# Output projection of the first batch's tokens at the end of the attention part, the rest in four banks

## The chip, the cores and the metric

The kernel runs on one core of one Trainium2 chip. The metric is the device time of one launch in microseconds; lower is better. The kernel before has a median of 1011.29 us over three runs (1010.05 to 1013.51).

## What is computed

One transformer layer on x of shape (2, 1024, 512): a layer norm, causal attention with 16 heads of 32, a mixture of 8 experts with the top 2 per token, and both results added to x. Cut to what matters here:

```python
xn = layernorm(x)
q, k, v = split(xn @ w_attn + b_attn); rope on q and k (by head index)
attn = softmax(where(causal, q @ k.T, -inf)) * 512 ** -0.5
a = (attn @ v) @ w_proj + b_proj                     # output projection
probs = softmax(xn @ gate_w.T); top 2 experts per token, weights normalised
f = sum over the two experts: w * (silu(g) * u) @ w2, with g, u = split(xn @ w1)
out = x + a + f
```

## The kernel before

The program has three parts, each a block: at the end of a block all five engines meet, and none starts the next part before the last has come.

`project_qkv` computes the layer norm, q, k, v and the router's choice and stores them in HBM. `attend` is the attention. It runs 16 rounds (`ROUNDS`), each for two heads of one batch: rounds 0 and 1 belong to batch 0, 2 and 3 to batch 1, and so on through four groups of heads; four heads of one batch make a span, of which there are 8 (`SPANS`). A round has 12 steps (`NS`); in each PE computes a block of transposed scores (`scores`), ACT takes the exponential into `probs`, and PE multiplies by the values (`values`) into `o_acc`. In steps 0 to 3 and 8 to 11 the block lies on the diagonal, and GpSimd sets what is above it to zero first (line 1137); the value product waits for that (`masked`). Beside this PE computes the scores once more for the round two ahead (`unit`), of which DVE takes the row maxima. SP issues all transfers of this part: the loads of q, k and v three rounds ahead (`load`, lines 1019 and 1023), the rows of maxima (`rows`, 1030), the sums and unscaled outputs of a finished round (`sort_out`, 1041 and 1045), and for each span the sums back in (`load_totals`, 1052), the shares, which DVE makes of them with a reciprocal (`share`, 1215), out (`store_shares`, 1056) and spread over partitions (`spread_shares`, 1064). GpSimd then scales the span's outputs in `o_t` (`scale_span`, 1129), in odd rounds behind the mask of step 3, and for the last span behind the last round. SP's order within a round is written out by hand: load, second half's `sort_out` of the round before, spreading, rows, totals, first half's `sort_out`, store of shares.

`experts` begins with the output projection. `o_t` holds the attention's output transposed, 16 token tiles of 128. For each tile `a` SP loads x's rows into one of 4 buffers `res` (708), GpSimd adds the bias (729), PE multiplies by `w_proj` in 4 steps, each two matmuls in the profile (887), into the bank `gu[a % 2][0]`, DVE adds the two (801) back into `o_t`, and SP stores that to `acc` in HBM (712). PE may start tile `a` when DVE is through with tile `a - 2`. ACT issues the weights of expert `e`, three transfers (788 to 790), when `3e - 1` tiles are done (16 at most):

```python
if e:
    act.wait_ge(res_done, min(3 * e - 1, NT))
if e == E - 2:
    rows_to_sbuf(0, 0)
```

ACT does its first expert work only behind the last of these issues. GpSimd waits for the weights of all 8 experts in turn (`expert_ready`), only then loads the first tag (`load_tag`, 737: a token's number and weight), and waits for the 16 stores before the first accumulation.

Then come 39 expert tiles (`SLOT_TILES`) of 128 routed rows: load of rows (702), transposition (PE 830, ACT 764), up projection (PE 835), silu (ACT 779), product (DVE 818), transposition (PE 845, DVE 808), down projection (PE 853), scaling by the tag (ACT 771), and accumulation into `acc` by an indirect DMA (747). Tile `i` of ACT starts with `y_to_sbuf(i - 2)`, which waits for tag `i - 2`, and ends with the silu of tile `i` and the rows of tile `i + 1`; PE turns the hidden values of tile `i - 1` within tile `i`. At the end SP copies `acc` to the output.

## Time and profile before

| | |
|---|---|
| median of three runs | 1011.29 us |
| profiled execution | 1012.41 us |
| its span, first to last instruction | 1010.8 us |
| PE busy | 881.2 us (87%) |
| DVE busy | 360.9 us (36%) |
| ACT busy | 291.1 us (29%) |
| GpSimd (POOL) busy | 282.7 us (28%) |
| mean granted clock of PE | 0.931 |
| moved by DMA | 143.12 MB, mean 142 GB/s |
| part 1, `project_qkv` | 0 to 190 us |
| part 2, `attend` | 190 to 608 us |
| part 3, `experts` | 608 to 1011 us, its projection to 668 us |

The profiled execution is 1.1 us above the median; its span leaves out 1.6 us around the first and the last instruction. Shares of busy time are means over the three parts, which have different limits, so the timeline and the stretches are to be read part by part. In the rows, SPq and ACTq are DMA issues by SP and ACT, PEld is PE's weight load, and what stands in brackets is the idle time before a group and what ended it.

### The profile page before, as it was taken

The page shows a single profiled execution, that of the slowest core. Times are in us where ns is not written, and L with a number is a line of the kernel's source. Part 1 is how long each engine was busy: PE and PEld are TensorE (multiplying, and loading weights), DVE is VectorE, ACT ScalarE, POOL GpSimd, SP SyncE. Part 2 cuts the span into 40 slices and gives each one's busy share as a digit, 9 for nine tenths or more (in the row PEclk, how much of TensorE's full clock was granted, in tenths as well). Part 3 has the DMA queues.
Part 4 walks back from the last instruction along what each step waited for, and adds up shares of the span by engine and source line. Part 5 has one row for each costly group of instructions (what it writes and reads, how often), then busy time and mean ns, then how long its engine had stood idle before and what let it go on. Part 6 is the DMA issues. An engine that isn't in the chain of part 4 may idle for free. (4 is left out here: it accounts for less than half of the span.)

```text
span 1010.8 us, 12520 instructions
## 1 busy us (share of the span) xinstructions
PE 881.2 (87%) x3533; PEld 524.8 (52%) x3534; DVE 360.9 (36%) x1086; ACT 291.1 (29%) x612; POOL 282.7 (28%) x363
## 2 busy tenths in 40 slices
PE   3899999375999889898989938999999999999990
PEld 2768778243554445455545413445566666656650
DVE  5853342572566555565655101111111111111110
ACT  2221121001465445454544620011222222222210
POOL 5732300466011221212122122413222333222231
PEclk9989999756799899999999978999999999999995
DMA  9296595998176554566651018994333333333326
GB/s 327 112 290 208 188 302 186 220 291 291 34 126 113 90 111 86 106 132 120 105 106 39 25 48 308 372 352 103 73 62 62 62 62 66 67 75 63 62 31 187
DMA packets 107415, 143.12 MB, mean 142 GB/s; under 512 B 46192, under 2 KB 54896, under 8 KB 107312
## 3 DMA queue, kind: packets, MB, share of 16 engines
q1 hardware_dynamic: 82864, 93.74, 36.3%
q0 software_dynamic: 9424, 18.69, 10.3%
q10 hardware_dynamic: 15088, 30.22, 9.0%
q8 instruction: 17, 0.28, 0.1%
q14 instruction: 22, 0.18, 0.1%
HBM read 79.11 MB, written 59.06 MB: 137 GB/s over the span
## 5 line engine op out<-in xcount | busy, mean ns | idle before, releaser
L1172 ACT ACTIVATE probs<-scores_t 128x512 f32<-128x512 f32 (+3 forms) x384 | 163.5, 490 | 149.6 <-PE scores_t L1280 127.5
L835 PE MATMUL gu<-w,rows_t 128*128 x624 | 197.6, 459 | 1.7 <-ACT rows_t L764 1.6
L1257 PE MATMUL maxima<-k_stack,q_stack 96*128 96x512 f32 (+3 forms) x384 | 145.1, 401 | 35.7 <-DVE row_lo L1207 19.8
L1298 PE MATMUL o_acc<-probs,v_ones 128*64 128x512 f32 (+3 forms) x768 | 152.2, 519 | 12.4 <-POOL probs L1137 12.4
L835 PEld LDWEIGHTS gu<-w,rows_t 128*128 128x128 f32 x624 | 115.0, 190 | 70.8 <-issue 21.1
L1280 PE MATMUL scores_t<-q_stack,k_stack 98*128 98x512 f32 (+3 forms) x384 | 141.9, 397 | 6.2 <-ACT probs L1172 3.3
L1193 DVE CUSTOM_DVE_ANT_0 masked_scores<-maxima,mask_m 128x128 f32<-128x128 f32 (+3 forms) x256 | 120.6, 486 | 38.7 <-PE maxima L1257 32.3
L1197 DVE TENSOR_REDUCE mx<-maxima 128x1 f32<-128x512 f32 x128 | 88.2, 689 | 115.4 <-PE maxima L1257 106.9
L1257 PEld LDWEIGHTS maxima<-k_stack,q_stack 96*128 96x128 f32 x384 | 80.1, 211 | 59.7 <-DVE row_lo L1207 24.4
L1280 PEld LDWEIGHTS scores_t<-q_stack,k_stack 98*128 98x128 f32 x384 | 75.1, 199 | 64.2 <-issue 45.3
L853 PE MATMUL down<-w,hidden_t 128*128 (+1 forms) x234 | 107.0, 592 | 0.8 <-DVE hidden_t L809 0.8
L1137 POOL TENSOR_SCALAR_AFFINE_SELECT probs<-probs 128x256 f32<-128x256 f32 x120 | 48.2, 408 | 192.8 <-ACT probs L1172 192.5
L1298 PEld LDWEIGHTS o_acc<-probs,v_ones 128*64 128x64 f32 x768 | 48.0, 140 | 80.6 <-issue 41.5
L808 DVE COPY hidden_t<-hid_ps 128x256 f32<-128x256 f32 x39 | 16.6, 425 | 178.6 <-PE hid_ps L845 178.6
L771 ACT ACTIVATE y<-down,tag 128x512 f32<-128x512 f32 x39 | 26.8, 687 | 184.2 <-PE down L853 153.0
L887 PE MATMUL gu<-w_proj,o_t 128*128 128x512 f32 x128 | 58.3, 617 | 18.3 <-POOL ident L724 17.9
L747 POOL DMA_INDIRECT acc<-y,tag x39 | 64.0, 1640 | 16.8 <-issue 16.5
L853 PEld LDWEIGHTS down<-w,hidden_t 128*128 128x128 f32 (+1 forms) x234 | 44.5, 190 | 46.4 <-issue 38.4
L746 POOL TENSOR_TENSOR carrier_y<-ident 128x1 f32<-128x1 f32 x39 | 7.4, 190 | 192.4 <-ACT y L771 192.4
L495 PE MATMUL bank<-xt_hi,w_hi 128*128 128x512 f32 x128 | 52.3, 408 | 4.8 <-DVE w_lo L355 4.8
L818 DVE TENSOR_TENSOR hidden<-gu,gated 128x352 f32<-128x352 f32 x39 | 20.5, 525 | 92.3 <-PE gu L835 84.2
L737 POOL DMA_DIRECT2D tag<-routed x39 | 46.1, 1182 | 23.9 <-DMA w<-in_w_t 23.9
(147 smaller groups left out, 860.3 us busy)
## 6 DMA issues: line engine op xcount, KB each, us to landing
w<-in_w_t ACTq DMA_DIRECT2D x8, 1408.0 KB, 7.4
routed<-blank_row ACTq DMA_DIRECT2D x20, 514.0 KB, 6.2
rows<-routed SPq DMA_DIRECT2D x39, 256.0 KB, 4.1
qk_hi<-st_hi SPq DMA_DIRECT2D x32, 256.0 KB, 4.2
qk_lo<-st_lo SPq DMA_DIRECT2D x32, 256.0 KB, 5.3
q_stack<-qk_hi SPq DMA_DIRECT2D x32, 256.0 KB, 4.3
k_stack<-qk_hi SPq DMA_DIRECT2D x32, 256.0 KB, 6.6
x_rows<-xn SPq DMA_DIRECT2D x4, 1024.0 KB, 5.1
```

Source lines behind the costliest of these rows:

```text
L495: nc.tensor.matmul(out, a_hi(k), b_hi(k), start=(k == 0), stop=False)
L747: pool.indirect_dma_start(out=scratch["acc"], out_offset=bass.IndirectOffsetOnAxis(ap=tag[:, r, 0:1].bitcast(U32), axis=0), in_=y[:, r, :] ...
L835: last = nc.tensor.matmul(gu[r][j][:, 0:I], rows_t[r][:, k * P:(k + 1) * P], w1[:, bass.ds(e, 1), k, j * I:(j + 1) * I].rearrange("p o n - ...
L853: last = nc.tensor.matmul(down[r][:], hidden_t[r][0:n, k, :], w2[0:n, bass.ds(e, 1), k, :].rearrange("p o n -> p (o n)"), start=(k == 0), ...
L887: last = nc.tensor.matmul(gu[a % 2][0][:], o_t[:, g, a * P:(a + 1) * P], wp[:, g, :], start=(g == 0), stop=(g == NG - 1))
L1137: nc.gpsimd.affine_select(out=p, in_=p, compare_op=ALU.is_ge, fill=0.0, base=0, pattern=[[0, PAIR], [1, P]], channel_multiplier=-1).then_i ...
L1172: nc.scalar.activation(probs[:, k % PR, h, 0:w], scores_t[e % RING][:, 0:w], ACT.Exp).then_inc(exp_done, 1)
L1193: nc.vector.tensor_tensor_reduce(out=masked_scores[bank][:, 0:w], in0=scores, in1=mask_m[:, CH - w:CH], scale=1.0, scalar=NEG, op0=ALU.add ...
L1197: nc.vector.tensor_reduce(to, scores, AX.X, ALU.max).then_inc(m_free, 1)
L1257: nc.tensor.matmul(mb[at % RING][:, 0:w], q_st[i][0:3 * HD, h, t * P:(t + 1) * P], k_st[i][0:3 * HD, h, c * CH:c * CH + w], start=True, st ...
L1280: last = nc.tensor.matmul(out[:, 0:w], k_st[i][0:STACK, h, j * P:(j + 1) * P], q_st[i][0:STACK, h, t0:t0 + w], start=True, stop=not diag)
L1298: last = nc.tensor.matmul(o_acc[c][2 * HD * h:2 * HD * (h + 1), CH - w:CH], v_st[i][:, j, h, :], probs[:, k % PR, h, 0:w], start=(j == 0), ...
```

## The change

The first batch's 8 token tiles (`EARLY`) are projected in `attend`, behind the last value products, into the six banks that scores and maxima used (`proj_banks`). They belong to spans 0, 2, 4 and 6, so PE waits for 7 scaled spans. The bias and x of this batch are loaded in round 7 (`ROUNDS // 2 - 1`) with two transfers on SP's queue; x goes over the place of the normalised rows, which have been scattered by then. GpSimd adds the bias to one tile in each of rounds 8 to 15, before step 4. DVE adds and SP stores each tile; the reciprocal of the last span comes behind DVE's first addition. In `experts` 8 tiles (`LATE`) are left, in four banks; all weights from expert 3 on are issued when all 8 are done.

```diff
@@ -39,6 +39,7 @@
 CLEAR_TILES = -(-SLOT_TILES // (NCH * CLEARS)) * NCH * CLEARS
+EARLY = S // P
 I_TILES = [(0, 128), (128, 128), (256, 96)]
...
@@ -645,6 +646,7 @@
         RES = 4
+        LATE = NT - EARLY
         res = m.sbuf("res", [P, RES, D], F32)
...
@@ -665,7 +667,8 @@
         tag_in = [m.sem(f"tag_in{r}") for r in range(2)]
-        acc_started, added, stored = m.sem("acc_started"), m.sem("added"), m.sem("stored")
+        acc_started = keep["acc_started"]
+        added, stored = m.sem("added"), m.sem("stored")
         carried = m.sem("carried")
...
@@ -703,13 +706,14 @@
             tile(1, 1, 0)
-            for a in range(NT + RES - 1):
-                if a < NT:
-                    sp.dma_start(res[:, a % RES, :], x_rows[a]).then_inc(res_in[a % RES], 16)
+            for a in range(LATE + RES - 1):
+                if a < LATE:
+                    sp.dma_start(res[:, a % RES, :], x_rows[EARLY + a]).then_inc(res_in[a % RES], 16)
                 if a >= RES - 1:
                     done = a - (RES - 1)
+                    at = EARLY + done
                     sp.wait_ge(res_done, done + 1)
-                    sp.dma_start(acc_rows[done], o_t[:, :, done * P:(done + 1) * P]).then_inc(acc_started, 16)
+                    sp.dma_start(acc_rows[at], o_t[:, :, at * P:(at + 1) * P]).then_inc(acc_started, 16)
             run_tiles(sp, tile, 2)
...
@@ -724,7 +728,7 @@
             pool.wait_ge(bp_in, 16)
-            for a in range(NT):
+            for a in range(LATE):
                 pool.wait_ge(res_in[a % RES], 16 * (a // RES + 1))
...
@@ -782,8 +786,8 @@
                 if e:
-                    act.wait_ge(res_done, min(3 * e - 1, NT))
-                if e == E - 2:
+                    act.wait_ge(res_done, min(3 * e - 1, LATE))
+                if e == E // 2:
                     rows_to_sbuf(0, 0)
...
@@ -794,11 +798,12 @@
         def _(dve):
-            for a in range(NT):
+            for a in range(LATE):
+                at = EARLY + a
                 dve.wait_ge(proj_full, a + 1)
                 dve.wait_ge(biased, a + 1)
 
-                nc.vector.tensor_tensor(o_t[:, :, a * P:(a + 1) * P], gu[a % 2][0][:].rearrange("p (g t) -> p g t", t=P),
+                nc.vector.tensor_tensor(o_t[:, :, at * P:(at + 1) * P], gu[a % 2][a // 2 % 2][:].rearrange("p (g t) -> p g t", t=P),
                                         res[:, a % RES, :].rearrange("p (g t) -> p g t", t=P), ALU.add).then_inc(res_done, 1)
...
@@ -868,7 +873,7 @@
                 else:
-                    pe.wait_ge(res_done, NT - 1 + i)
+                    pe.wait_ge(res_done, LATE)
                 pe.wait_ge(expert_ready, e + 1)
...
@@ -878,13 +883,14 @@
             pe.wait_ge(ident_done, 1)
-            for a in range(NT):
-                if a >= 2:
-                    pe.wait_ge(res_done, a - 1)
-                if a == NT - 1:
+            for a in range(LATE):
+                at = EARLY + a
+                if a >= 4:
+                    pe.wait_ge(res_done, a - 3)
+                if a == LATE - 1:
                     turn_rows(0, 0, 0)
                 for g in range(NG):
-                    last = nc.tensor.matmul(gu[a % 2][0][:], o_t[:, g, a * P:(a + 1) * P], wp[:, g, :],
+                    last = nc.tensor.matmul(gu[a % 2][a // 2 % 2][:], o_t[:, g, at * P:(at + 1) * P], wp[:, g, :],
                                             start=(g == 0), stop=(g == NG - 1))
...
@@ -953,10 +959,14 @@
         o_t = keep["o_t"]
+        res = keep["x_rows"][:, 0:EARLY, 0:D]
+        bp = m.sbuf("bp_early", [P, D], F32)
 
         scores_t = [m.psum(f"scores_t{r}", [P, CH]) for r in range(RING)]
         o_acc = [m.psum(f"o_acc{c}", [P, CH]) for c in range(NC)]
         mb = [m.psum(f"maxima{r}", [P, CH]) for r in range(RING)]
+
+        proj_banks = scores_t + mb
 
...
@@ -976,6 +986,9 @@
         scaled = m.sem("o_scaled")
+        bp_in, res_in, biased = m.sem("bp_early_in"), m.sem("res_early_in"), m.sem("biased_early")
+        proj_full, res_done = m.sem("proj_early_full"), m.sem("res_early_done")
+        acc_rows = scratch["acc"][0:T, :].rearrange("(a p) (g t) -> a p g t", p=P, t=P)
         LOADS = 6 + PAIR
...
@@ -1068,6 +1081,10 @@
             for n in range(ROUNDS):
+                if n == ROUNDS // 2 - 1:
+                    sp.wait_ge(scattered, 16 * TOPK * NT)
+                    sp.dma_start(bp[:], b_proj.partition_broadcast(P)).then_inc(bp_in, 16)
+                    sp.dma_start(res, x[0].rearrange("(a p) d -> p a d", p=P)).then_inc(res_in, 16)
                 if n + SETS - 1 < ROUNDS:
...
@@ -1085,6 +1102,9 @@
             spread_shares(SPANS - 1)
+            for a in range(EARLY):
+                sp.wait_ge(res_done, a + 1)
+                sp.dma_start(acc_rows[a], o_t[:, :, a * P:(a + 1) * P]).then_inc(keep["acc_started"], 16)
 
...
@@ -1138,6 +1158,12 @@
                         scale_span(n // PAIRS - 1)
+                    if k == TPC and n >= ROUNDS - EARLY:
+                        a = n - (ROUNDS - EARLY)
+                        if a == 0:
+                            pool.wait_ge(bp_in, 16)
+                            pool.wait_ge(res_in, 16)
+                        nc.gpsimd.tensor_tensor(res[:, a, :], res[:, a, :], bp[:], ALU.add).then_inc(biased, 1)
             scale_span(SPANS - 1)
...
@@ -1233,7 +1259,13 @@
                     join(n + UNITS_AHEAD)
-            share(SPANS - 1)
+            for a in range(EARLY):
+                dve.wait_ge(proj_full, a + 1)
+                dve.wait_ge(biased, a + 1)
+                nc.vector.tensor_tensor(o_t[:, :, a * P:(a + 1) * P], proj_banks[a % len(proj_banks)][:].rearrange("p (g t) -> p g t", t=P),
+                                        res[:, a, :].rearrange("p (g t) -> p g t", t=P), ALU.add).then_inc(res_done, 1)
+                if a == 0:
+                    share(SPANS - 1)
 
...
@@ -1331,6 +1363,19 @@
                         values(n, k)
+
+            pe.wait_ge(w_proj_in, 16)
+            pe.wait_ge(scaled, SPANS - 1)
+            pe.wait_ge(exp_done, ROUNDS * NS * PAIR)
+            pe.wait_ge(m_free, ROUNDS * NU)
+            pe.wait_ge(row_lo_done, ROUNDS)
+            for a in range(EARLY):
+                if a >= len(proj_banks):
+                    pe.wait_ge(res_done, a - len(proj_banks) + 1)
+                for g in range(NG):
+                    last = nc.tensor.matmul(proj_banks[a % len(proj_banks)][:], o_t[:, g, a * P:(a + 1) * P], keep["w_proj"][:, g, :],
+                                            start=(g == 0), stop=(g == NG - 1))
+                last.then_inc(proj_full, 1)
 
...
@@ -1353,6 +1398,7 @@
             "tile_expert": m.sbuf("tile_expert", [1, SLOT_TILES], I32),
+            "acc_started": m.sem("acc_started"),
         }
```

On SP, from the store of shares in round 6 to the sums of round 6 in round 7, behind which comes the spreading of shares, it is now (before, without the rows of lines 1086 and 1087):

```order
L1069 DMA shares_all<-shares 128x32
L1086 DMA bp_early<-in_b_proj 128x512
L1087 DMA x_rows<-in_x 128x8x512
L1032 DMA q_stack2<-qk_hi 32x2x1024
L1032 DMA q_stack2<-qk_lo 32x2x1024
L1032 DMA q_stack2<-qk_hi 32x2x1024
L1032 DMA k_stack2<-qk_hi 32x2x1024
L1032 DMA k_stack2<-qk_lo 32x2x1024
L1032 DMA k_stack2<-qk_hi 32x2x1024
L1036 DMA v_ones2<-v_all 128x8x32 x2
L1054 DMA totals_all<-stage1 1x512 x2
L1058 DMA o_t<-stage1 32x512 x2
```

The load of the bias (1086) and of x (1087) have come between the store of shares and the loads of round 7's set.

On GpSimd, from the scaling in round 7 on, there was before:

```order
L1129 TENSOR_TENSOR o_t<-o_t,share_rows 128x1024
L1137 AFFINE_SELECT probs<-probs 128x2x128 x16
L1129 TENSOR_TENSOR o_t<-o_t,share_rows 128x1024
L1137 AFFINE_SELECT probs<-probs 128x2x128 x4
L1129 TENSOR_TENSOR o_t<-o_t,share_rows 128x1024
```

and there is now, where 1157 are the masks, 1149 is the scaling of a span and 1166 the addition of the bias:

```order
L1157 AFFINE_SELECT probs<-probs 128x2x128 x8
L1166 TENSOR_TENSOR x_rows<-x_rows,bp_early 128x512
L1157 AFFINE_SELECT probs<-probs 128x2x128 x8
L1149 TENSOR_TENSOR o_t<-o_t,share_rows 128x1024
L1166 TENSOR_TENSOR x_rows<-x_rows,bp_early 128x512
L1157 AFFINE_SELECT probs<-probs 128x2x128 x8
L1166 TENSOR_TENSOR x_rows<-x_rows,bp_early 128x512
L1157 AFFINE_SELECT probs<-probs 128x2x128 x8
L1149 TENSOR_TENSOR o_t<-o_t,share_rows 128x1024
L1166 TENSOR_TENSOR x_rows<-x_rows,bp_early 128x512
L1157 AFFINE_SELECT probs<-probs 128x2x128 x8
```

One addition stands in the middle of the masks of each even round, and one right behind the scaling of each odd round, in front of four masks.

On PE, from the last value products of attention to the first transposition of rows, there was before:

```order
L1298 MATMUL o_acc<-probs,v_ones 64x256 x2
L1298 MATMUL o_acc<-probs,v_ones 64x128 x2
L936 UNCONDITIONAL_BRANCH
L823 UNCONDITIONAL_BRANCH
L887 MATMUL gu<-w_proj,o_t 128x512 x60
L830 MATMUL turn_ps<-ident,rows 128x128 x4
L887 MATMUL gu<-w_proj,o_t 128x512 x4
```

and there is now:

```order
L1330 MATMUL o_acc<-probs,v_ones 64x256 x2
L1330 MATMUL o_acc<-probs,v_ones 64x128 x2
L1376 MATMUL scores_t<-w_proj,o_t 128x512 x12
L1376 MATMUL maxima<-w_proj,o_t 128x512 x12
L1376 MATMUL scores_t<-w_proj,o_t 128x512 x8
L942 UNCONDITIONAL_BRANCH
L828 UNCONDITIONAL_BRANCH
L893 MATMUL gu<-w_proj,o_t 128x512 x28
L835 MATMUL turn_ps<-ident,rows 128x128 x4
L893 MATMUL gu<-w_proj,o_t 128x512 x4
L864 TENSOR_LOAD tile_expert
L864 ISA x2
```

Half of the projections have gone ahead of the two jumps that lead into the next block, and the crossing between the parts now lies in the middle of them.

## Rows read from the trace of the kernel before

**Rows 1.** timeline, end of attention and projection: start, us, engine, line, what [idle before]

```profile
588.83 2.38 PE L1298 MATMUL o_acc<-probs,v_ones 128*64 128x512 f32 x16
...
602.83 2.34 POOL L1129 TENSOR_TENSOR o_t<-o_t,share_rows 128x1024 f32<-128x1024 f32 x1 [13.14 <-DMA share_rows<-shares_all]
...
608.36 0.82 SPq L702 DMA_DIRECT2D rows<-routed  x2
...
609.06 9.83 PE L887 MATMUL gu<-w_proj,o_t 128*128 128x512 f32 x16 [17.86 <-POOL ident L724]
...
617.26 1.26 POOL L729 TENSOR_TENSOR res<-res,bp 128x512 f32<-128x512 f32 x1 [8.25 <-DMA res<-in_x]
...
619.38 44.90 PE L887 MATMUL gu<-w_proj,o_t 128*128 128x512 f32 x104 [0.49 <-DVE o_t L801]
...
623.83 0.52 SPq L712 DMA_DIRECT2D acc<-o_t  x1
```

**Rows 2.** stretches: width, busy us by engine, granted clock, DMA share, GB/s

```profile
404.00:406.00 2.00, 2.00 (x18) 1.45 (x16) 1.97 (x9) 1.16 (x5) 0.81 (x2) 1.00 0.16 51
...
424.00:426.00 2.00, 2.00 (x6) 0.76 (x3) 0.00 (x0) 0.03 (x1) 0.00 (x0) 0.50 0.00 0
...
620.00:630.00 10.00, 10.00 (x25) 4.47 (x24) 2.10 (x4) 0.00 (x0) 3.95 (x4) 1.00 1.05 372
```

**Rows 3.** DMA, 609 to 687 us: forty rates; SP's queue (packets, MB, time share)

```profile
GB/s 153 164 397 411 394 384 328 371 395 398 350 372 390 374 399 367 371 340 397 403 370 352 300 385 400 399 371 173 334 402 385 255 343 394 402 360 356 396 386 82
...
q1 hardware_dynamic: 11472, 9.70, 37.5%
```

**Rows 4.** timeline of all engines, 672 to 696 us

```profile
672.06 0.51 ACTq L790 DMA_DIRECT2D w<-in_w_t  x1
...
678.92 0.66 PE L830 MATMUL turn_ps<-ident,rows 128*128 128x128 f32 x4 [0.91 <-DMA rows<-routed]
...
687.96 0.62 POOL L737 DMA_DIRECT2D tag<-routed  x1 [23.90 <-DMA w<-in_w_t]
...
691.91 0.53 DVE L818 TENSOR_TENSOR hidden<-gu,gated 128x352 f32<-128x352 f32 x1 [4.03 <-ACT gated L779]
...
695.15 0.49 PE L845 MATMUL hid_ps<-ident,hidden 128*128 128x128 f32 x3
```

**Rows 5.** PE's timeline, rounds 7 and 13 of attention

```profile
422.64 2.57 PE L1298 MATMUL o_acc<-probs,v_ones 128*64 128x512 f32 x8 [2.29 <-POOL probs L1137]
...
553.60 1.72 PE L1298 MATMUL o_acc<-probs,v_ones 128*64 128x512 f32 x8
```

**Rows 6.** waits of the whole span: total us, times, longest

```profile
PE o_acc L1298 <- POOL probs L1137: 12.4, 5, 2.9
```

**Rows 7.** SP's queue in the timeline, round 7

```profile
401.11 0.35 SPq L1056 DMA_DIRECT2D shares_all<-shares  x1
...
408.57 4.34 SPq L1041 DMA_DIRECT2D totals_all<-stage  x2
...
414.27 3.20 SPq L1064 DMA_DIRECT2D share_rows<-shares_all  x4
```

**Rows 8.** GpSimd's timeline, rounds 12, 13 and 15

```profile
529.68 0.41 POOL L1137 TENSOR_SCALAR_AFFINE_SELECT probs<-probs 128x256 f32<-128x256 f32 x1 [10.18 <-ACT probs L1172]
...
550.32 0.77 POOL L1137 TENSOR_SCALAR_AFFINE_SELECT probs<-probs 128x256 f32<-128x256 f32 x2
...
586.74 0.41 POOL L1137 TENSOR_SCALAR_AFFINE_SELECT probs<-probs 128x256 f32<-128x256 f32 x1 [0.32 <-ACT probs L1172]
```

**Rows 9.** SP's queue in the timeline, end of the first part

```profile
186.38 0.38 SPq L205 DMA_DIRECT2D qk_lo<-st_lo  x1
...
190.17 0.35 SPq L1019 DMA_DIRECT2D q_stack<-qk_hi  x1
```

**Rows 10.** SP's own waits: total us, times, longest

```profile
SPq L209 <- DMA qk_lo<-st_lo: 2.5, 1, 2.5
```

**Rows 11.** one line, the issue of w2: ns min/median/max

```profile
L789 ACTq DMA_DIRECT2D w<-in_w_t x8: 527/531/1104, 609.3 to 670.9; - x8
```

4 lines of the change are left out of this document (2 added, 2 removed).

## Prediction

> **What bounds the kernel now.** The page names TensorE (PE) as the busiest engine; the chain that ended last, followed back from the end, is PE in the expert tiles and, before them, PE in the output projection. Its slices of the DMA engines, though, are as full in the projection. So I split the part around the change into stretches and asked of each what ends last, in the timeline of every engine.
>
> *The end of the attention part.* PE finishes the last value products at 588.83 + 2.38 = 591.21 us and starts the projection at 609.06: idle for 17.86 us. In that time a chain of short transfers runs (sums out, totals in, a reciprocal, shares out and back), GpSimd scales the last span from 602.83 to 605.17, and the expert part begins 3.2 us later, at 608.36. The first 16 projection matmuls take 9.83 us, the next 104 take 44.90, 0.432 each (6.9 for 16) [rows 1]. The granted clock is 1.00 (2.4 GHz) later [rows 2]; that the first 16 are slower fits half of it.
>
> *The projection, 609 to 668 us.* PE never idles, but the DMA engines are full too: 372 GB/s at a share over 1 [rows 2]. From 609 to 687 us the forty rates average 350 GB/s, 27.3 MB [rows 3], most of it expert weights on ACT's queue. GpSimd sees the last weights only at 687.96. Behind that wait it loads the first tag; then ACT makes the first y and the gated values of tile 2, DVE its hidden values at 691.91 + 0.53 = 692.4, and PE turns those at 695.15 [rows 4]. So PE is 2.7 us from being held by the weights. This decides the change: half of the projection may leave this stretch of PE, but the weights don't land sooner by that.
>
> *The attention part.* In odd rounds GpSimd waits for the shares' transfer and releases the masks late, so that PE idles: 2.29 us in round 7 [rows 5], five times in all (rounds 3, 5, 7, 9, 11), 12.4 us, up to 2.9 [rows 6]. In round 13, without loads, PE takes its masks at 553.60 with no wait [rows 5].
>
> **Part 1, loading x and the bias in round 7.** SP now issues 0.26 MB of bias and 2.10 MB of x right behind the shares' store (401.11 + 0.35), ahead of the round's loads, on the same queue. At 372 GB/s these 2.36 MB take 6.3 us. The loads' bytes begin to move at about 406.2: up to 406 the DMA share is 0.16 [rows 2]. The new transfer starts at about 403.2 (1.7 us behind its issue, as I read for the loads) and ends at 409.5: the loads are late by 3.3 us. Behind them stand the sums of round 6, whose issue even now takes 4.34 us, and the spreading of the shares at 414.27 [rows 7], for which GpSimd waits, for whose masks PE waits. PE is already idle there, so all of it is paid: **+3.3 us**. Ends: 0, if the transfers share the engines without loss, and 6.3, if nothing falls in the idle gap. No row has 2 MB ahead of a load; the nearest is the sums' 4.34 us, and it shows a queue that goes in order. The Trainium skill, page "DMA: Bandwidth & Descriptors", section "Queues, rings and completion order", says that each engine takes the descriptors of one queue in ring order; by it nothing passes and the term is 3.3, and if transfers of one queue took turns it would be near 0.
>
> **Part 2, eight bias additions on GpSimd in rounds 8 to 15,** each 1.26 us as in the expert part [rows 1]. In even rounds they lie in the 10.18 us in which GpSimd waits for exponentials: 0. In rounds 9 and 11 one stands between the scaling and masks that PE already waits for: 1.26 each, **+2.5 us**. In round 13 the first two masks end at 551.1, with the addition 552.4, and PE takes them at 553.60: 0. In round 15 they end at 587.15, then at 588.4, against PE's 588.83: 0 [rows 8, 5, 1]. Ends: 0 and 5.0 (all four odd rounds).
>
> **Part 3, the first batch's projection behind the value products.** 8 token tiles of 8 matmuls at 0.432 us: 27.6 us, at full clock, since PE comes from work at 1.00. In the times of before it runs from 591.3 to 618.9. Its last store is issued 1.5 us later, at 620.4 (as now: the third tile ends at 619.38 + 8 x 0.432 = 622.8, its store's issue at 623.83 + 0.52 [rows 1]). The chain of short transfers runs beside it and is done at 605.17; DVE's reciprocal stands behind only the first addition, which ends before the totals arrive. The crossing to the expert part takes between 1.0 us, as at the first one of the program, where SP came last (186.76, 2.5 us of waiting for a transfer, start at 190.17) [rows 9, 10], and 3.2 us (behind GpSimd). SP comes last now: 1.0, and a start at 621.4, **13.0 us later**.
>
> **Part 4, from the start of the expert part to the landed weights.** Before: 687.96 - 608.36 = 79.6 us. Removed: 16 transfers of 256 KB, 4.19 MB. By bytes at 372 GB/s that is 11.3 us; by the time share of SP's queue (37.5% of 78 us for 9.70 MB [rows 3]) 12.7. I take 12.0. Besides, the rates dip twice late (173 and 255 among 390s [rows 3]), where ACT waits for projected tiles before it issues the next expert; now experts 3 to 7 are issued in one go, about 650: -1.3. **-13.3 us**. Ends: -11 (bytes alone) and -17 (the 23.1 MB left at 395 GB/s, and 4.4 us of start and landing). The same page of the Trainium skill ("DMA: Bandwidth & Descriptors", section "Where 436 GB/s comes from") gives about 358 GB/s as the limit of a core's HBM; by it 23.1 MB take 64.5 us and the term is -10.7. This trace moves 372 [rows 2], so the rows decide.
>
> **Part 5, from the landed weights to the turn of tile 2's hidden values.** Before: 7.2 us. PE is now through with its half at 622.1 + 27.6 = 649.7 (times of before) and far ahead; it must wait 10 us or more and comes out at half clock: +2.9 us, as behind the gap of 17.86 us (9.83 - 6.9); even round 7's 2.29 us are followed by 0.50, 1.2 GHz [rows 2]. If only the tag chain holds PE, the turn comes at 4.5 + 2.9 = 7.4. But ACT issues all weights before its first expert work, and its queue took 1.10 us for an issue that else takes 0.53, with two experts in flight [rows 11]. With five in flight its last issue slips, to about 15 us before the landing (before: 687.96 - 672.57 = 15.4 [rows 4]). From that issue to the turn are now 22.6 us, less 1.3 of waits for rows (0.91 at 678.92 [rows 4], the rest in restarts), plus 2.9 of clock: the turn is at 9.2. Between 7.4 and 9.2 I take 8.2: **+1.0 us**. The tiles after it follow as before.
>
> The four banks save one PE stall of 0.49 us [rows 1], under part 4's cover: 0.
>
> **Sum:** 3.3 + 2.5 + 13.0 - 13.3 + 1.0 = +6.5 us. The profiled execution is 1012.41 us (span 1010.8) and would be 1018.9. The median of the runs is 1011.29, 1.1 lower: I forecast 1017.8.
>
> **Rivals.**
> A, faster. The weights were paced by ACT's waits, not by the engines, and issued in one go they flow faster. To make up for the other parts (3.3 + 2.5 + 13.0 + 1.0 = 19.8) they must land 59.8 us behind the start; less 4.4 of start and landing that is 23.1 MB in 55.4 us, 417 GB/s on average: from there it decides. At 445 the part is 56.3 us, the sum -3.5, the time 1007.8. For it: the dips, and a slice at 411 [rows 3]. Against: a share over 1 at 372 [rows 2]. Chance 0.10.
> B, the expert part pays too. ACT's queue holds only two experts (4.2 MB), so its last issue comes 10.8 us at 390 GB/s plus 2 of landing before the weights are in, and the turn 24.2 - 12.8 = 11.4 behind them, +3.2; with a crossing of 3.2 us +5.4, 1023.2. It decides once the last issue is less than 16.8 us (21.3 - 4.5) before the landing. Chance 0.14.
> C, no change. The queue of round 7 mixes without loss (0) and part 4 gives -15: +1.5, 1012.8. Chance 0.14.
> My forecast: 0.62.
>
> **How the numbers follow.** A measurement of this kernel tells about 0.3% (3.0 us) from no change. B and the forecast lie above 1014.3, save 0.04 of the forecast. Slower 0.72, same 0.18 (C and those 0.04), faster 0.10 (A). The range 1012.5 to 1024 takes in part 1 from 0 to 6.3, part 4 from -11 to -17 (one at an end, the others near their values) and most of B; it leaves out A, some of C and of B, 2 in 10.
>
> **What would show it.** Round 7: shares spread at about 417.6, and PE's stall grows from 2.29 to about 5.6 us. Rounds 9 and 11: stalls longer by 1.3 each. Value products end at about 597 and the early projection runs unbroken at clock 1.00. GpSimd's wait for weights ends at about 693.5, and PE idles 10 us or more in expert tiles 0 to 2, with clock 0.50 behind it. I am wrong if the loads of round 7 aren't late, if GpSimd's masks still come in time, or if the weights land before 690.

## The result, and the profile after

| | before | after |
|---|---|---|
| median of the runs beside each other | 1011.62 us (1010.05 to 1013.51) | 1028.21 us (1022.38 to 1033.28) |
| ratio, 95% interval | | 1.016, 1.013 to 1.019 |
| profiled execution | 1012.41 us | 1022.38 us |
| its span | 1010.8 us | 1020.7 us |
| mean granted clock of PE | 0.931 | 0.929 |

The change makes the kernel slower by 16.6 us. I had forecast 1017.8 (+6.5) with a range up to 1024: the direction was right, the size was not. A second set of runs of the same kernel on another chip gave 1.014 (below). The profiled execution of after is the fastest of its four, so its trace shows 9.9 of the 16.6 us. Up to round 7, where nothing is changed, it is already 3.5 us ahead of the trace of before (the loads behind round 6 start at 401.05, against 404.56). Read against that point, its parts add to 13.0 us; in the second trace of the same kernel, below, the same parts add to 16.7.

Line numbers of after are higher than those of before: L1330 is the value product (L1298), L1157 the mask (L1137), L741 the tag (L737).

**Round 7.** SyncE's queue in the timeline of after:

```profile
398.49 0.43 SPq L1087 DMA_DIRECT2D x_rows<-in_x  x1
401.05 0.34 SPq L1032 DMA_DIRECT2D q_stack<-qk_hi  x1
...
404.14 7.20 SPq L1036 DMA_DIRECT2D v_ones<-v_all  x2
411.38 3.24 SPq L1054 DMA_DIRECT2D totals_all<-stage  x2
414.66 3.19 SPq L1058 DMA_DIRECT2D o_t<-stage  x2
417.96 1.91 SPq L1077 DMA_DIRECT2D share_rows<-shares_all  x4
...
431.76 0.34 SPq L1032 DMA_DIRECT2D q_stack<-qk_hi  x1
```

in that of before, the first loads of this round and of the next:

```profile
404.56 0.34 SPq L1019 DMA_DIRECT2D q_stack<-qk_hi  x1
...
428.69 0.34 SPq L1019 DMA_DIRECT2D q_stack<-qk_hi  x1
```

the forty rates of after, 394 to 424 us (a slice is 0.75 us):

```profile
GB/s 0 27 74 98 3 3 51 169 202 156 101 232 317 399 401 401 404 366 224 205 219 219 235 240 229 237 188 150 98 96 62 68 131 101 175 262 175 27 49 118
```

and GpSimd and PE of the same round:

```profile
422.72 2.34 POOL L1149 TENSOR_TENSOR o_t<-o_t,share_rows 128x1024 f32<-128x1024 f32 x1 [19.81 <-DMA share_rows<-shares_all]
```

```profile
425.47 3.25 PE L1330 MATMUL o_acc<-probs,v_ones 128*64 128x512 f32 x8 [8.64 <-POOL probs L1157]
```

The bias and x move at 400 GB/s only in the second half of their time. From 399.25 to 403.0 the slices are 169, 202, 156, 101 and 232; at 407.5 the rate falls to 205 to 240, which is what the round's own loads also had before (180 to 280). The slices from 399.25 to 407.5 add to 2.36 MB, the bias and x alone. So the loads behind them begin at about 407.5, where on these times (3.5 us ahead) they would have begun at 402.0: 5.5 us late and not 3.3. SP stands in its issues meanwhile: the two of the values' load take 7.20 us, where they take 1.07 in the trace of before. The shares' spreading is issued at 417.96, before at 414.27 in a round that began 3.5 us later [rows 7]: 7.2 us late. PE's stall is 8.64 us where it was 2.29 [rows 5], and the round takes 30.7 us where it took 24.1: **+6.6 us**, of which I had half.

Two windows of after, during the stall and behind it (width, busy us of PE, PEld, DVE, ACT, POOL, granted clock, DMA share, GB/s):

```profile
422.00:425.00 3.00, 0.00 (x0) 0.00 (x0) 0.00 (x0) 0.00 (x0) 2.28 (x1) 0.50 0.19 46
428.00:430.00 2.00, 2.00 (x9) 1.18 (x6) 0.33 (x1) 0.56 (x2) 0.00 (x0) 0.70 0.00 0
```

The clock is at 0.50 (1.2 GHz) while PE is idle, and the eight value products at 425.47 take 3.25 us where at 1.00 they take 1.72 [rows 5]. Half clock stands in this trace from 419 to 429, 10.2 us; before, from 423 to 427, 3.4 us.

**Rounds 9 and 11.** GpSimd's timeline of after, round 9:

```profile
466.91 2.35 POOL L1149 TENSOR_TENSOR o_t<-o_t,share_rows 128x1024 f32<-128x1024 f32 x1 [13.03 <-DMA share_rows<-shares_all]
469.22 1.09 POOL L1166 TENSOR_TENSOR x_rows<-x_rows,bp_early 128x512 f32<-128x512 f32 x1
470.26 1.49 POOL L1157 TENSOR_SCALAR_AFFINE_SELECT probs<-probs 128x256 f32<-128x256 f32 x4
```

The addition stands between the scaling and the masks, 1.09 us (forecast 1.26). Rounds 9 and 11 take 0.9 and 1.3 us more: +2.2, forecast +2.5.

**The crossing.** Timeline of after, from the last value products to the expert part:

```profile
596.47 10.57 PE L1376 MATMUL scores_t<-w_proj,o_t 128*128 128x512 f32 x24
...
605.71 19.76 SPq L1107 DMA_DIRECT2D acc<-o_t  x8
...
607.90 2.35 POOL L1149 TENSOR_TENSOR o_t<-o_t,share_rows 128x1024 f32<-128x1024 f32 x1 [12.87 <-DMA share_rows<-shares_all]
...
626.12 0.20 POOL L726 MEMSET ident<- 128x128 f32 x1 [15.88 <-POOLq L942]
```

The projection runs unbroken at clock 1.00, 0.43 us a matmul. The scaling is over at 610.25 and GpSimd then waits 15.88 us for the others; the last store's issue ends at 605.71 + 19.76 = 625.47, and the next part starts 0.65 us later. From the values' end (596.53) to the start are 29.6 us, against 17.1 [rows 1]: +12.4, forecast +13.0.

**From the start to the landed weights.** The forty rates of after, 626 to 695.5 us (a slice is 1.74 us), and then GpSimd, DVE and the queues around 657 us:

```profile
GB/s 174 202 231 394 409 395 391 316 305 395 400 393 353 372 411 406 396 389 268 15 182 402 396 402 353 397 391 391 312 400 392 305 380 392 361 325 402 388 245 14
```

```profile
657.56 1.26 POOL L733 TENSOR_TENSOR res<-res,bp 128x512 f32<-128x512 f32 x1 [4.29 <-DMA res<-in_x]
658.93 0.69 DVE L806 TENSOR_TENSOR o_t<-gu,res 128x512 f32<-128x512 f32 x1 [4.86 <-POOL res L733]
659.65 0.42 ACTq L792 DMA_DIRECT2D w<-in_w_t  x1
...
695.46 0.62 POOL L741 DMA_DIRECT2D tag<-routed  x1 [36.64 <-DMA w<-in_w_t]
```

The engines run dry: 268, 15, 182. The weights of expert 3 wait for eight projected tiles. PE is through with its half at 656.7, 30.6 us behind the start where I had 28.3; it came out of the crossing at half clock (mean 0.83 from 626 to 636). The last rows of x land later still: the loads take 10.0 us from issue to landing, and GpSimd waits for the last one until 657.56. So DVE's eighth addition is at 658.93 and the issue at 659.65, 33.5 us behind the start. I had put it at about 650 with a start of 621.4, 28.6 us behind. The weights are seen at 695.46: 69.3 us behind the start of the part, where before they took 79.6. **-10.3, forecast -13.3.**

**From the landed weights to tile 2.** ScalarE's timeline of after:

```profile
664.52 3.51 ACTq L793 DMA_DIRECT2D w<-in_w_t  x1
668.06 2.45 ACTq L794 DMA_DIRECT2D w<-in_w_t  x1
...
671.20 3.20 ACTq L793 DMA_DIRECT2D w<-in_w_t  x1
674.43 2.38 ACTq L794 DMA_DIRECT2D w<-in_w_t  x1
...
677.49 3.00 ACTq L793 DMA_DIRECT2D w<-in_w_t  x1
680.53 0.49 ACTq L794 DMA_DIRECT2D w<-in_w_t  x1
681.05 1.28 ACT L783 ACT_TABLE_LOAD   x1 [19.21 <-issue]
```

and PE's:

```profile
683.51 5.06 PE L840 MATMUL gu<-w,rows_t 128*128 x8 [13.02 <-ACT rows_t L768]
...
704.65 0.49 PE L850 MATMUL hid_ps<-ident,hidden 128*128 128x128 f32 x3
```

ACT's issues, 0.53 us when the queue is free [rows 11], stand up to 3.51 us. The last ends at 681.02, 14.4 us before the landing (forecast 15), and only then ACT makes its first expert work; PE has waited 13.02 us for it and comes out at half clock (5.06 us for what takes 2.53 a little later). The turn of tile 2's hidden values is 9.2 us behind the landed weights, 7.2 before: +2.0, forecast +1.0. From there to the end both traces take about 316 us.

The five differences are 6.6 + 2.2 + 12.4 - 10.3 + 2.0 = 12.9; the distances measured directly, 8.8 (rounds 7, 9, 11) and 4.2 (values' end to turn of tile 2: 108.1 against 103.9), give 13.0.

### The profile page after: what moved, and what is told of

It is laid out like the page before. It is cut to its first block and busy times, and to the rows that moved or that the text cites. A ratio compares the mean times of both kernels' runs of the same rounds, so it can differ in the third digit from the quotient of the medians.

```text
span 1020.7 us, 12517 instructions
## 1 busy us (share of the span) xinstructions
PE 882.5 (86%) x3533; PEld 524.3 (51%) x3534; DVE 360.1 (35%) x1086; ACT 291.0 (29%) x612; POOL 281.8 (28%) x363
## 5 line engine op out<-in xcount | busy, mean ns | idle before, releaser
L840 PE MATMUL gu<-w,rows_t 128*128 x624 | 202.7, 468 | 18.4 <-ACT rows_t L768 18.4
L1330 PE MATMUL o_acc<-probs,v_ones 128*64 128x512 f32 (+3 forms) x768 | 153.8, 524 | 19.8 <-POOL probs L1157 19.8
L840 PEld LDWEIGHTS gu<-w,rows_t 128*128 128x128 f32 x624 | 117.5, 194 | 89.1 <-issue 40.6
L1312 PE MATMUL scores_t<-q_stack,k_stack 98*128 98x512 f32 (+3 forms) x384 | 139.6, 391 | 3.3 <-ACT probs L1198 3.3
L1219 DVE CUSTOM_DVE_ANT_0 masked_scores<-maxima,mask_m 128x128 f32<-128x128 f32 (+3 forms) x256 | 120.5, 485 | 34.0 <-PE maxima L1289 28.6
L1157 POOL TENSOR_SCALAR_AFFINE_SELECT probs<-probs 128x256 f32<-128x256 f32 x120 | 48.2, 408 | 184.0 <-ACT probs L1198 183.7
L1330 PEld LDWEIGHTS o_acc<-probs,v_ones 128*64 128x64 f32 x768 | 48.6, 142 | 88.9 <-issue 41.7
L813 DVE COPY hidden_t<-hid_ps 128x256 f32<-128x256 f32 x39 | 16.6, 425 | 183.5 <-PE hid_ps L850 183.5
L823 DVE TENSOR_TENSOR hidden<-gu,gated 128x352 f32<-128x352 f32 x39 | 20.5, 525 | 106.2 <-PE gu L840 76.6
L741 POOL DMA_DIRECT2D tag<-routed x39 | 46.1, 1181 | 36.6 <-DMA w<-in_w_t 36.6
L296 ACT ACTIVATE st_hi<-bank,small 128x512 fp32r<-128x512 f32 x32 | 21.8, 688 | 105.0 <-PE bank L498 100.1
```

The source lines that it names most:

```text
L741: pool.dma_start(tag[:, r:r + 1, :], in_rows[bass.ds(i, 1), :, D:XW].rearrange("a p d -> p a d")).then_inc(tag_in[r], 16)
L840: last = nc.tensor.matmul(gu[r][j][:, 0:I], rows_t[r][:, k * P:(k + 1) * P], w1[:, bass.ds(e, 1), k, j * I:(j + 1) * I].rearrange("p o n - ...
L1157: nc.gpsimd.affine_select(out=p, in_=p, compare_op=ALU.is_ge, fill=0.0, base=0, pattern=[[0, PAIR], [1, P]], channel_multiplier=-1).then_i ...
L1219: nc.vector.tensor_tensor_reduce(out=masked_scores[bank][:, 0:w], in0=scores, in1=mask_m[:, CH - w:CH], scale=1.0, scalar=NEG, op0=ALU.add ...
L1312: last = nc.tensor.matmul(out[:, 0:w], k_st[i][0:STACK, h, j * P:(j + 1) * P], q_st[i][0:STACK, h, t0:t0 + w], start=True, stop=not diag)
L1330: last = nc.tensor.matmul(o_acc[c][2 * HD * h:2 * HD * (h + 1), CH - w:CH], v_st[i][:, j, h, :], probs[:, k % PR, h, 0:w], start=(j == 0), ...
```

## The experiments

Each was timed in turns with the kernel before, four kernels to a set: its median was 1013.45, 1000.76 and 1000.56 us in the three sets; where it isn't 1013.45, it is named. Only ratios are compared across sets. The sets ran on different chips, and most of the 13 us between their medians shows in one place: round 0 of attention, unchanged in every kernel here, takes 41 to 46 us in the traces of before, of after and of the first set, and 32 to 34 in those of the other two.

**The same kernel again.**

> The changed kernel once more, for a second profile and more times, because its four runs lie between 1022 and 1033 us and the profiled one is the lowest. Theory L (the cost is a lengthening of fixed places): stall of round 7 about 8.6 us, start of the expert part to the last weights seen about 69 us, from there to the turn of tile 2's hidden values about 9.2 us, as in the first profile, and the spread comes from the unchanged part before round 7, which was some 3.5 us early in the first profile; the median should then be near 1026. Theory V (one of the new places is unstable): one of these three numbers differs by 3 us or more from the first profile.

Measured 1027.28 us, ratio 1.014 (1.011 to 1.018). Its trace repeats the places: stall of round 7 8.31 us, values' end to start 29.6, start to landed weights 70.3, landing to turn 8.1. What varies is the clock behind the stall of round 9. The window 470 to 484 of the first trace of after, and then of this one:

```profile
470.00:484.00 14.00, 12.68 (x61) 6.86 (x62) 6.50 (x23) 6.08 (x15) 4.62 (x10) 0.88 0.46 110
```

```profile
470.00:484.00 14.00, 13.54 (x42) 6.95 (x43) 4.81 (x15) 3.44 (x8) 4.34 (x10) 0.52 0.32 75
```

The half clock lasts 3.4 us there and 13.7 here, with the same code. That is one source of the spread of 11 us between the runs of after. Against the trace of before, round 7 is 6.3 us longer here, rounds 8 to 11 another 6.3 (2.2 in the first trace) and the stretch from the values' end to the turn 4.0: with rounding 16.7 us.

**The attention side alone.** The kernel before, with the loads in round 7 and the eight additions; the projection stays where it was and adds the bias and x again by itself, so the eight additions are made in vain.

```diff
+                if n == ROUNDS // 2 - 1:
+                    sp.dma_start(bp[:], ...)
+                    sp.dma_start(res, x[0]...)
...
+                        nc.gpsimd.tensor_tensor(res[:, a, :], res[:, a, :], bp[:], ALU.add)...
```

> The kernel before with only the loads of bias and x in round 7 and the eight additions on GpSimd; the whole projection stays in the expert part. Theory L: +6.5 us from round 7's stall (8.6 in place of 2.3) and +2.2 from rounds 9 and 11, so about 1020. Rival D (what happens in attention is made up later, the expert part sets the cost): 1012 to 1014.

Measured 1023.93, ratio 1.0105 (1.007 to 1.014): +10.5 us, three quarters of the 13.8 that the changed kernel loses in the same set, without moving one matmul. PE's timeline, round 7, and then round 9:

```profile
430.88 3.25 PE L1312 MATMUL o_acc<-probs,v_ones 128*64 128x512 f32 x8 [8.26 <-POOL probs L1145]
...
476.78 3.15 PE L1312 MATMUL o_acc<-probs,v_ones 128*64 128x512 f32 x8 [3.29 <-POOL probs L1145]
```

Values' end to turn is 104.6 us, the 103.9 of before: the expert side is untouched.

**The loads alone.** As the last, without the additions.

> The kernel before with nothing added but the load of x's first batch (2 MB) and of the bias in round 7; nothing reads them and no addition is made. The run with loads and additions cost +10.5 us. If the stand of the SyncE queue behind the 2 MB load is the attention side's price by itself: round 7 takes 30 to 31 us where it takes 24, the PE's wait for the masks in it 8 to 9 us where it was 2.29, and the whole +6 to +8 us (ratio 1.006 to 1.008). If the additions carry half of it, as my sum had it (3.3 for the loads): the wait in round 7 is at most 6 us and the whole +3 to +4. Rounds 9 and 11 keep the stalls of the kernel before (1.95 and 2.94).

Measured 1008.3 against 1000.56, ratio 1.007 (1.004 to 1.010): +7 us. SyncE's queue and PE in round 7:

```profile
396.34 7.56 SPq L1027 DMA_DIRECT2D v_ones<-v_all  x2
403.94 2.69 SPq L1045 DMA_DIRECT2D totals_all<-stage  x2
406.68 3.88 SPq L1049 DMA_DIRECT2D o_t<-stage  x2
```

```profile
417.87 3.25 PE L1308 MATMUL o_acc<-probs,v_ones 128*64 128x512 f32 x8 [8.88 <-POOL probs L1145]
```

Round 7 takes 31.0 us, and rounds 9 and 11 keep stalls of 1.61 and 2.96 us. So the loads make round 7 6.8 us longer by themselves, not my 3.3. The additions are then the rest; the two traces put them at 1.7 + 1.3 = 3.0 in the stalls of rounds 9 and 11 (3.29 and 4.25 with them).

**The loads late.** The changed kernel with the loads in round 13, behind the last round's rows of maxima, and the additions behind the last masks.

```diff
-                if n == ROUNDS // 2 - 1:
+                if n == ROUNDS - 3:
                     sp.dma_start(bp[:], ...)
                     sp.dma_start(res, x[0]...)
...
-                    if k == TPC and n >= ROUNDS - EARLY:
-                        nc.gpsimd.tensor_tensor(res[:, a, :], ...)
+            for a in range(EARLY):
+                nc.gpsimd.tensor_tensor(res[:, a, :], ...)
             scale_span(SPANS - 1)
```

> The changed kernel with the two loads put off to round 13, which loads nothing else, behind its rows of maxima, and the eight additions behind the last masks. Theory L: stalls of rounds 7, 9 and 11 as in the kernel before (2.3, 1.9, 2.9), none in rounds 13 and 15, 8.8 us less than the changed kernel. Rival D: no more than 2 us less.

Measured 1018.41, ratio 1.0047 (1.002 to 1.007): +5.0 us. The stalls of rounds 7, 9 and 11 are 3.16, 1.77 and 2.44, as before the change. All eight additions, 9.14 us on GpSimd, fit ahead of the last scaling. What is left is the expert side: +12.4 to the start, -9.2 to the landed weights (70.4), +2.6 to the turn of tile 2. Two thirds of the loss (8.8 of 13.8 us) were thus avoidable by place alone. The two sides taken singly, 10.5 and 5.0, add to more than the 13.8, by less than their intervals.

**ScalarE's first tiles between the weights' issues.** The changed kernel; ACT does tile 0 ahead of the issues of expert 5 and tile 1 ahead of those of expert 6.

```diff
+                if e == E // 2 + 1:
+                    tile(0, 0, 0)
+                if e == E // 2 + 2:
+                    tile(1, 1, 0)
                 act.dma_start(w1[:, e], ...)
...
-            run_tiles(act, tile)
+            run_tiles(act, tile, 2)
```

> The changed kernel with ACT's work of expert tiles 0 and 1 placed ahead of the weight issues of experts 5 and 6. Theory Q (ACT's full queue holds its first silu until 14 us before the last weights land): the silu of tile 0 comes near 664 in place of 682 us, the turn of tile 2's hidden values comes 7 to 7.5 us behind the last weights in place of 9.2, total 2 us less. Rival T (the tag behind all weights sets it, the queue hides under it): the turn stays 9 us behind the weights, total the same. If the issues of experts 6 and 7 are now late and the engines run dry, the weights land later and it is slower.

Measured 1024.35, ratio 1.012 (1.008 to 1.016). ScalarE and PE in its timeline:

```profile
669.54 0.46 ACT L783 ACTIVATE gated<-gu 128x352 f32<-128x352 f32 x1
...
700.46 0.69 ACT L775 ACTIVATE y<-down,tag 128x512 f32<-128x512 f32 x1 [25.36 <-DMA tag<-routed]
```

```profile
702.21 4.67 PE L844 MATMUL gu<-w,rows_t 128*128 x8 [14.71 <-ACT rows_t L768]
```

The first silu is at 669.54, not 682.34, but the third tile still waits for the tag, which is loaded behind the landed weights: the turn is 8.3 us behind the landing (9.2 and 8.1 in the two traces of after). Theory Q had 7 to 7.5 and rival T 9. On these traces the ACT queue and the tag hold to almost the same time, so that taking one away gave no more than 1 us.

**The scaling off the masks' way.** The kernel before, with the scaling of each span moved from the odd round, where the masks of step 8 stand behind it, to the next even round.

```diff
-                    if k == TPC - 1 and n % PAIRS == 1 and n > PAIRS:
-                        scale_span(n // PAIRS - 1)
+                    if k == TPC - 1 and n % PAIRS == 0 and n > PAIRS:
+                        scale_span(n // PAIRS - 2)
+                    if k == TPC - 1 and n == ROUNDS - 1:
+                        scale_span(n // PAIRS - 1)
```

> The kernel before with the scaling of spans 0 to 5 moved from step 3 of odd rounds to step 3 of the even round behind. Theory S (PE's stalls in the odd rounds cost their own length and as much again or more in half clock behind them, and are what part 1 and 2 lengthened): rounds 3, 5, 7, 9 and 11 take 20.2 us in place of 23.7 to 25.4, so about 20 us less than before. Rival M (masks would be late anyway, by ACT): less than 5 us.

Measured 979.34 against 1000.76, ratio 0.9775 (0.971 to 0.984): 21.4 us faster, with nothing of the change under study. PE in round 7, at the products that stood there before, and GpSimd's scaling, now in round 8:

```profile
399.07 1.73 PE L1300 MATMUL o_acc<-probs,v_ones 128*64 128x512 f32 x8
```

```profile
405.42 2.37 POOL L1129 TENSOR_TENSOR o_t<-o_t,share_rows 128x1024 f32<-128x1024 f32 x1
```

No wait for masks is left, and from 300 to 555 us the mean granted clock is 1.00. Rounds 3, 5, 7, 9 and 11 take 101.2 us together; in the trace of before they take 122.3, 21.1 more. The stalls in them are only 12.4 us [rows 6], but the trace of before also stands 20.5 us at half clock in these rounds, and this one not at all. So a stall that I priced at its length costs more than its length.

**The same with the change.**

> The changed kernel with the same move of the scaling. Theory S: the load of x in round 7 still makes the spreading of shares 6 us late, but nobody waits for that now, and the additions in odd rounds stand before masks that are not late; so the difference to the run with the scaling moved in the kernel before is only the expert part's 4 to 5 us, not 14. Rival P (the load itself, through the queue, holds something else up in round 7 or 8): the difference stays over 8 us.

Measured 993.8 against 1000.76, ratio 0.9915 (0.989 to 0.994). Against the run above the change costs 14 us here too, as rival P had it, though PE no longer waits for a mask. PE's timeline shows why:

```profile
404.15 0.79 PE L1314 MATMUL scores_t<-q_stack,k_stack 98*128 98x512 f32 x1 [4.46 <-DMA q_stack<-row_lo]
```

SP issues the last rows of maxima of round 8 at 401.67, 19.4 us into round 7 where it is 13.4 in the run above, and PE waits 4.46 us for them. Round 7 takes 26.9 us where 20.2 is the length without a stall: +6.6 again. Round 8 takes 1.9 us more, and the values' end to the turn of tile 2 another 5.0 (109.6 against 104.6): 13.5 of the 14.5 us. There were two waits behind the queue, and the first hid the second.

**Tags ahead of the weights' wait.** The changed kernel; GpSimd loads tags 0 and 1 before it waits for the weights, and ACT does three tiles between the issues.

```diff
             load_tag(0, 0)
+            load_tag(1, 1)
+            for e in range(E):
+                pool.wait_ge(weights_in[e], 3 * 16)
+                pool.sem_inc(expert_ready, 1)
...
+                if e == E // 2 + 3:
+                    tile(2, 0, 1)
```

> The changed kernel with the first two tags loaded before GpSimd waits for the weights, and ACT's expert tiles 0, 1 and 2 placed between the issues of experts 4 to 7. Theory W (in the changed kernel PE has 20 us and more in hand in the expert part, and only the waits for the last weights, by the tag and by ACT's queue, keep it from using them): PE turns the hidden values of tile 2 before the last weights land, and the gate moves to tile 4, 16.2 us later in PE's order: 11 to 16 us less than the changed kernel. Rival R (the rows of tiles 2 and 3, on SP's queue behind ten megabytes of weights, come late and hold PE): no more than 5 us less.

Measured 1007.94 against 1000.76, ratio 1.008 (1.005 to 1.012). The turn of tile 2 is now ahead of the landing (676.87 against 685.98), and the wait goes to tile 4, where PE stands 8.56 us, both as theory W had it. But start to turn of tile 4 is 90.0 us, against 94.7 in after: some 5 us gained, not 11 to 16. What holds tile 4 is shown under the next run.

**All four moves together:** late loads, scaling moved, tags ahead, three tiles between the issues.

> All of it in the changed kernel: scaling in even rounds, x and bias loaded in round 13 and added behind the last masks, two tags ahead, ACT's tiles between the issues. Theories S and W together: attention 20 us shorter than before, expert part 10 us shorter than in the changed kernel and some 6 to 10 shorter than before: 980 to 990 us.

Measured 979.25 against 1000.76, ratio 0.978 (0.972 to 0.984): the same as the scaling's move alone (979.34). GpSimd and PE in its timeline:

```profile
658.77 0.18 POOL L746 TENSOR_TENSOR carrier_y<-ident 128x1 f32<-128x1 f32 x1 [37.68 <-DMA w<-in_w_t]
...
666.36 1.18 POOL L737 DMA_DIRECT2D tag<-routed  x1
...
672.28 4.80 PE L846 MATMUL gu<-w,rows_t 128*128 x8 [8.51 <-ACT rows_t L768]
```

The tag of tile 2 comes behind two accumulations, and those behind the landing at 658.8; PE waits again, and again comes out at half clock (4.80). Against the scaling's move alone the expert part starts 12.0 us later (587.1 and 575.1), and from its start to the turn of tile 4 it takes 14.0 us less (89.8 and 103.8): the one eats the other.

**Weights issued sooner.** The changed kernel; experts 1 to 4 at 2, 4, 6, 8 projected tiles in place of 2, 5, 8, 8.

```diff
-                    act.wait_ge(res_done, min(3 * e - 1, LATE))
+                    act.wait_ge(res_done, min(2 * e, LATE))
```

> The changed kernel; ScalarE issues the weights of experts 1, 2, 3, 4 at 2, 4, 6, 8 finished projections where it was 2, 5, 8, 8. Theory: the weights land 69 to 70 us behind the crossing and not the forecast 66.3 because expert 3's issue stands until the eighth projection's addition (33.5 us in) and the DMA engines run dry for about 3 us there. Then the dry slice (14 to 18 GB/s) goes, the last weights land 2 to 3 us earlier behind the crossing (66.5 to 67.5), and the time falls by 1 to 3 us against the changed kernel. Rival: the rows of x and the stores of sums take their share of the same engines and only wait longer behind the weights, so that the dry slice only moves (the last rows of x land later, the eighth addition with them) and the landing stays at 69 to 70: no difference. With the weights' landing unchanged the turn of tile 2 stays 9 us behind it.

Measured 1011.28 against 1000.56, ratio 1.009 (1.006 to 1.012). The forty rates from the start of the expert part, 616.6 to 686 us:

```profile
GB/s 197 188 232 407 400 396 391 304 271 343 389 397 348 328 394 400 401 382 404 402 395 372 287 310 404 397 354 336 391 394 296 337 400 364 267 396 394 300 103 1
```

The dry slices are gone, and the weights are seen 67.6 us behind the start (684.26; 69.3 and 70.3 in the two traces of after). So the gap cost some 2 to 3 us, and without it the stretch is 12.0 us shorter than before. The turn is 9.6 us behind the landing, 9 as expected. Start to turn is shorter by 1.3 us than in after. The ratio is 0.5% below that of the changed kernel run again, more than the trace shows, but the two intervals overlap; that difference stays unclear.

**Four tiles in place of eight.** The kernel with late loads, and `EARLY = 4`: four tiles behind the value products, twelve in the expert part.

```diff
-EARLY = S // P
+EARLY = 4
...
+                    sp.dma_start(res, x[0, 0:EARLY * P]...)
```

> Four tiles of tokens are projected behind the last value products and twelve in the expert part; loads in round 13 and additions behind the last masks, as in the run with the late load (1.0047). Theory: the projection of eight tiles (27 us of PE) delays the crossing by 12.5 us because only some 14 us of it lie beside the last shares' scaling; four tiles (13 us) fit beside it, so that the values' end to the crossing falls from 29.6 to 17 to 19 us (17.1 before), while the expert part's start to landed weights is 74 to 76 us (between 79.6 with sixteen tiles there and 70 with eight). Sum against the kernel before: +0.5 -4.5 and +1 for the ACT queue, -2 to -5 us (ratio 0.995 to 0.998). If instead the crossing is held by the stores or the DMA of the shares and not by PE's products, it stays above 25 us and the time is that of eight tiles or worse (+5 or more).

Measured 995.6 against 1000.56, ratio 0.9934 (0.991 to 0.996): **faster than before**. The timeline from the projection's start to the next part:

```profile
577.82 10.57 PE L1374 MATMUL scores_t<-w_proj,o_t 128*128 128x512 f32 x24
...
587.07 6.02 SPq L1107 DMA_DIRECT2D acc<-o_t  x4
...
589.34 2.35 POOL L1149 TENSOR_TENSOR o_t<-o_t,share_rows 128x1024 f32<-128x1024 f32 x1 [8.40 <-DMA share_rows<-shares_all]
...
594.86 0.20 POOL L726 MEMSET ident<- 128x128 f32 x1 [3.18 <-POOLq L942]
```

The stores are issued by 593.09, the scaling ends at 591.69, and the crossing takes 16.96 us, as before the change (17.1): four tiles fit beside the transfers of the shares, eight don't. Weights land 74.3 us behind the start, about halfway between sixteen tiles (79.6) and eight (70.4 with late loads). Values' end to turn is 100.0 us, against 103.9 before and 109.7 with eight tiles and late loads.

**Four tiles and all moves.**

> As the run with all moves (scaling off the masks' way, late load, tags ahead, three ScalarE tiles between the issues), with four tiles in the tail in place of eight. That run took 0.978 of the kernel before, the scaling moved alone the same. Theory: the crossing comes 9 to 11 us earlier than with eight tiles, the landing of the weights 4 to 5 us earlier, and the whole is 4 to 6 us faster than with eight: ratio 0.972 to 0.975. If the gate behind the weights is the tags' queue and the first ScalarE tiles alone, whose distance to the landing is fixed, the whole follows the landing all the same; if the loads of late rows land later than before (res rows behind the weights), the landing stays and the ratio is 0.977 to 0.979.

Measured 968.92 against 1000.56, ratio 0.967 (0.964 to 0.971), the best of the study. GpSimd and PE:

```profile
648.27 0.18 POOL L746 TENSOR_TENSOR carrier_y<-ident 128x1 f32<-128x1 f32 x1 [28.00 <-DMA w<-in_w_t]
...
661.72 5.06 PE L846 MATMUL gu<-w,rows_t 128*128 x8 [3.68 <-ACT rows_t L768]
```

The weights land at 648.3, 73.6 us behind the start, only 1.9 more than with eight tiles (71.7) while the start is 12.4 us earlier; I had allowed 4 to 6 us for the whole and got 10.3 by the medians. PE's wait at tile 4 falls from 8.51 to 3.68. How much of the distance to the scaling's move alone (979.34) comes from the four tiles and how much from the tags and ScalarE's tiles was not taken apart.

## Why the prediction was wrong in size

**Part 1, +3.3, measured +6.6 and +6.3 in the two traces of after, +6.8 with the loads alone.** The step that failed is "At 372 GB/s these 2.36 MB take 6.3 us" with the 3.3 that follows from it. The place, the order and the chain (sums, shares, masks, PE) were right. But the rate of the projection doesn't hold in the first 3 to 4 us of this transfer (100 to 230 GB/s), so that it holds the queue for about 8 us (399.3 to 407.5), and the round's own loads start 0.7 us earlier than I read (405.5 in the trace of before, not 406.2). Late by 5.5, not 3.3. Another 1.1 comes on the way to the end of the round: the spreading is 7.2 late, the masks 6.4. SP's long stand in its issues lies there, but no run takes it apart from the bytes; x on another queue or in smaller pieces was not tried. My upper end of 6.3, "if nothing falls in the idle gap", was nearly the truth. The Trainium skill's page "DMA: Bandwidth & Descriptors", section "Queues, rings and completion order", has the descriptors of one ring taken in order. The rates agree: what moves from 399.3 to 407.5 is 2.36 MB, which leaves nothing for the round's loads.

**Part 2, +2.5, measured +2.2 in the trace, about 3.0 between the two runs of before with and without the additions.** Right in place and size, for the stalls. In the second trace of after rounds 8 to 11 cost 6.3 us, because the half clock behind the stall of round 9 lasts longer (see "What wasn't in the sum").

**Part 3, +13.0, measured +12.4.** Right: SP comes last, and the crossing behind it is short (0.65 us, forecast 1.0).

**Part 4, -13.3, measured -10.3 (-9.3 in the second trace).** The 12.0 us for the bytes were right: with weights issued sooner the part is 12.0 us shorter. The step that failed is "now experts 3 to 7 are issued in one go, about 650: -1.3". The issue came 659.65 - 626.12 = 33.5 us behind the start, 4.9 later than I had it: 2.3 of these because PE came out of the crossing at half clock, the rest behind the last rows of x, which land late behind the weights. The 1.3 us that I hoped to save with the dips didn't come, and one dry gap took 2 to 3 us more. The same page of the Trainium skill, section "Where 436 GB/s comes from", gives about 358 GB/s for a core's HBM, by which the term was -10.7. That is near the measured value, but not for its reason: from 662 to 690 us the trace of after moves 375 GB/s, above that figure, and the time is lost between 658 and 662, where it moves 91.

**Part 5, +1.0, measured +2.0 (+0.9 in the second trace).** The mechanism was right: the last issue ends 14.4 us before the landing against my 15, and the turn is at 9.2, the upper end of my own sum, and 8.1. Rival B had 12.8 and a turn at 11.4; neither that turn nor its crossing of 3.2 us came. That B's 1023.2 lies nearer to the measured time than my 1017.8 is luck.

**What wasn't in the sum.** The step that failed here is that PE's stalls were taken at their length, and the half clock behind them at nothing outside part 5. From round 7 to the values' end the trace of before stands 10.2 us at half clock, the first trace of after 20.5, the second 27.3. The first costs 8.8 us there and the second 12.7, with stalls of the same length (15.0 and 15.2 us in rounds 7, 9 and 11). That difference of 3.8 is the one between the 13.0 and the 16.7 us of the two traces, and the medians, 13.8 and 16.6 slower, lie between. The scaling's move shows the same from the other side: 12.4 us of waits gone, 21.4 us gained. Why the half clock behind one stall lasts 3.4 us in one execution and 13.7 in another stays open.

So of the 10 us between +6.5 and +16.6, part 1 is 3, part 4 is 3, part 5 is 1, and up to 4 are this half clock; parts 2 and 3 give nearly 1 back.

The rivals: A (faster) needed 417 GB/s on average for 23.1 MB, and by the same reckoning (69.3 us less 4.4) the trace of after has 356. C needed round 7 to cost nothing. Both fell. My range let one term be at its end with the others near their values. Part 1 came out past its upper end and part 4 past its own (-10.3 against -11) at once; with part 5 that gives 1024.2 even without the half clock.

## What to carry to other kernels

A large transfer ahead of small ones on a queue delays all of them and holds the issuing engine too: look for every later issue of that engine and for whom each feeds (here the second waiter showed only when the first was gone), and put the transfer where the queue has nothing urgent. Work moved into a gap is free only up to the gap's length: four tiles (13.8 us) fit the 17 us crossing and gained, eight (27.6) moved the crossing by 12.4 and lost. And where a late engine's stall is small but repeated, price it with the clock behind it: moving one GpSimd instruction out of the masks' way gave 21.4 us, where the projection's move in its better form, four tiles with late loads, gave 5.0.

## What the runs showed of the hardware

- An issue of a 0.5 MB weight transfer that takes 0.53 us on a free queue stood up to 3.51 us on ACT (4.39 in the run with sooner weights). The last one ended 14.4 us before the landing. In that time the DMA engines moved 4.5 MB in all (313 GB/s), so at most two experts' weights (2.1 MB each) were still to land. On SP two issues together stood 7.20 us behind 2.1 MB of x.
- The length of the half clock behind a stall differs between executions of one kernel: behind the stall of round 9, about 3 us each time, it is 3.4 us in one trace of after and 13.7 in the other. With the stall of 8 to 9 us in round 7 it was 10.2 in all seven traces that have that stall; it began some 2 us into the stall and ended some 4 us behind it.
- A crossing between two parts takes 0.65 us behind the end of SP's last issue when that comes last, and 3.2 us behind GpSimd's last operation when that does (3.2 before the change, 3.17 with four tiles, where SP's last issue had ended 1.8 us before the start).
